# A two-layer gated cross-attention and top-2 expert kernel: expert blocks that start beside the tail of the routing

## The chip, the cores and the metric

One core of one Trainium2 chip runs the whole program. The metric is device time in microseconds of one execution. A profile of one execution gives the time of every instruction on TensorE (PE, its weight loads PEld), VectorE (DVE), ScalarE (ACT), GpSimd (POOL) and of the DMAs that SyncE (SP) and POOL issue.

## What is computed

The input x has 2,048 tokens (8 batches of 256) of width 256; each batch has 120 context rows. Two layers follow each other, cut here to what matters:

```python
for l in range(2):
    x = x + tanh(g_xattn[l]) * cross_attention(layernorm(x), ctx)   # 16 heads of depth 16
    h = layernorm(x)
    w, idx = top_k(softmax(h @ router_w[l]), 2)                     # 8 experts, 2 for each token
    # layer 0: experts silu(h @ gate) * (h @ up) @ down, hidden 688
    # layer 1: experts square(relu(h @ w1)) @ w2, hidden 256
    x = x + tanh(g_ffn[l]) * sum(w[k] * expert[idx[k]](h) for k in range(2))
```

## The kernel before, in words

All arithmetic is f32, but for the rank products and some mask products in bf16. Each layer has an attention part, then an expert part.

**Attention** runs over 16 units (`u`, half a batch of 128 queries each; `G = 16 l + u`). In a unit PE makes the query-ordered scores of the next unit (`scores`), DVE takes row maxima of them (`row_max`, `split_max`, line 841), PE makes the key-ordered scores less the maxima (`shifted`, L1265, L1270), ACT takes their exponent (L647, L649), PE multiplies with the values (`values`, L1291, in two halves), DVE turns and divides (`divide`, L858 to L869), PE projects (`out_proj`, L1299, L1300), DVE adds to x and takes statistics (`residual`, L875 to L881), POOL and ACT normalize (L514 to L519, L657).

**Routing** follows a few units behind: PE transposes the normalized rows (`x2_t`, L1306), ACT copies them out (L663), PE makes 8 logits for each token (`route`, L1312), and for a batch (two units) DVE finds the two experts (`route1`, L893 to L910), PE counts ranks within each expert (`ranks`, L1319 to L1328), DVE makes the row of each token (`route2`, L916 to L930), and POOL scatters the rows of x to a buffer in HBM sorted by expert (`scatter`, L544, four DMAs of a batch). The scatter of batch b stands in POOL's order at unit 2(b+3).

**The list of blocks.** The expert part works through 39 blocks of 128 sorted rows. After the batches 0 to 5 (`EARLY = 6`) `N1 = 17` blocks are sure to be full, whatever the last two batches bring; `list_full` (14 DVE instructions, L995 to L1024) lists their rows and weights, and stands behind the attention loop. `list_rest` lists the other 22 beside the first blocks. The rows between the end of an expert's rows and the next multiple of 128 are filled by eight pad writes (L410), which need the final counts.

**A block** is: SP loads 128 rows (`load_block`, L397, L398, into one of three buffers), PE transposes them (`block_t`, L1468), DVE copies them out (`x_evac`, L1115, L1118), PE multiplies up (`up`, L1482), ACT and DVE apply the nonlinearity (L723 and L1145 in layer 0, L742 and L1172 in layer 1), PE transposes (L1495, L1503) and multiplies down (`down`, L1512), the result is copied out (L1129 or L737), and POOL stores it to the row of each token (`store_block`, L551). The three buffers make the load of block j wait for the transposes of block j-3. At the end of a layer SP reads the results back and DVE adds them to x (`combine`, L825).

Every engine works through its instructions in the order in which they are written; semaphores alone tie the engines together. Between the attention loop and the first block every engine has a piece of code of its own for the last units: on PE, behind the loop (`G1` is the last unit, `B1` the last batch):

```python
route(G1 - 2, 5); x2_t(G1 - 1); out_proj(G1); ranks(B1 - 1)
route(G1 - 1, 7); x2_t(G1); route(G1, 0); ranks(B1)
...
block_t(0)
run_blocks(l, (blk0, blk1)[l])
```

and SP waits for the list, for the scatters of batches 0 to 5 and then loads three blocks. The last expert's weights of layer 0 (slot 7 of `w_all`, where keys and values lie during attention) are loaded once `values` of the last unit is done.

## Time and profile before

| | us |
|---|---|
| median of 3 timed runs (762.58 to 766.7) | 766.17 |
| the profiled execution, its time | 769.0 |
| its span in the profile | 767.3 |
| PE busy | 678.0 (88%) |
| DVE busy | 415.0 (54%) |
| ACT busy | 274.4 (36%) |
| POOL busy | 214.4 (28%) |
| mean granted TensorE clock, share of full | 0.952 |

The span is the time from the first to the last record. Busy shares are averages over parts with different limits, so the two changes from attention to experts have to be read in the timeline, by the waits that end last there. TensorE's clock has two levels here, 2.4 GHz (1.00 in the views) and 1.2 GHz (0.50).

### The profile page before, as it was taken

What the parts mean: (1) busy time and instruction counts of PE and PEld (TensorE: products, weight loads), DVE (VectorE), ACT (ScalarE), POOL (GpSimd) and SP (SyncE); (2) the same over time, 40 slices, a digit from 0 to 9 for tenths busy, and PEclk for the clock granted to TensorE, in tenths of its full rate; (3) what the DMA queues carried; (4) which work ended last, traced back from release to release, by engine and by line L of the source; (5) the groups of instructions that cost most, each with busy time, mean ns of one, the idle gap of its engine ahead of it and who ended that gap; (6) DMA issues with size and microseconds to landing.
All of it is one profiled execution on the core that took longest, in us unless ns stands there. A gap on an engine that the chain in (4) does not pass through costs nothing.

```text
span 767.3 us, 17444 instructions
## 1 busy us (share of the span) xinstructions
PE 678.0 (88%) x5804; PEld 520.4 (68%) x5804; DVE 415.0 (54%) x1385; ACT 274.4 (36%) x528; POOL 214.4 (28%) x399
## 2 busy tenths in 40 slices
PE   5798999859999999999999999978888885999970
PEld 3666767637777777777777777657666663788850
DVE  4777888753333333233332332469989876454426
ACT  3556576411211112112111112256555541354530
POOL 4122553460111111111111011212355436344440
PEclk9999999859999999999999999999999986899995
DMA  9044554461131131111011010320112122544428
GB/s 218 18 144 138 182 179 141 148 220 43 56 101 51 36 79 35 35 32 39 28 35 36 29 28 21 143 92 29 58 64 70 64 85 78 151 125 121 123 83 328
DMA packets 50856, 70.71 MB, mean 92 GB/s; under 512 B 7687, under 2 KB 38023, under 8 KB 50771
## 3 DMA queue, kind: packets, MB, share of 16 engines
q1 hardware_dynamic: 42380, 50.85, 22.1%
q0 software_dynamic: 6816, 18.69, 6.9%
q8 instruction: 51, 0.84, 0.5%
q10 hardware_dynamic: 1575, 0.05, 0.1%
q14 instruction: 34, 0.28, 0.1%
HBM read 46.55 MB, written 23.02 MB: 91 GB/s over the span
## 4 chain that ended last, share of the span: by engine, by line
PE 69%; DVE 18%; issue 5%; DMA 4%; POOL 2%; ACT 2%; DVEq 0%; SPq 0%; POOLq 0%; ACTq 0%
PE ps L1482 28%; PE ps L1512 17%; PE ps L1299 4%; DVE m_rows L841 4%; PE ps L1495 3%; DVE x_sb L825 3%; PE ps L1312 2%; PE ps L1237 2%; DVE ctx_q L858 2%; PE ps L1468 2%; PE ps L1291 2%; DMA ys_dram<-share,dest_i 2%; PE ps L1265 2%; PE ps L1254 1%; DVE x_sb L875 1%
## 5 line engine op out<-in xcount | busy, mean ns | idle before, releaser
L1482 PE MATMUL ps<-w_all,share 128*128 x780 | 232.4, 446 | 4.2 <-DVE share L1118 4.2
L1482 PEld LDWEIGHTS ps<-w_all,share 128*128 128x128 f32 x780 | 146.9, 193 | 66.5 <-issue 8.4
L551 POOL DMA_INDIRECT ys_dram<-share,dest_i x78 | 75.9, 974 | 333.2 <-DVE share L1129 279.8
L1512 PE MATMUL ps<-w_all,share 112*128 (+1 forms) x624 | 147.9, 380 | 1.7 <-ACT share L737 1.0
L1512 PEld LDWEIGHTS ps<-w_all,share 112*128 112x128 f32 (+1 forms) x624 | 112.4, 190 | 15.1 <-issue 2.6
L1145 DVE TENSOR_TENSOR share<-share,ps 128x344 f32<-128x344 f32 x78 | 40.0, 513 | 140.5 <-PE ps L1482 79.3
L726 ACT COPY share<-ps 128x512 f32<-128x512 f32 x39 | 22.9, 587 | 151.9 <-PE ps L1495 151.9
L841 DVE TENSOR_REDUCE m_rows<-ps 128x8 f32<-128x960 f32 x64 | 70.4, 1139 | 11.0 <-PE ps L1254 10.9
L723 ACT ACTIVATE share<-ps 128x344 f32<-128x344 f32 x78 | 35.9, 460 | 106.9 <-PE ps L1482 106.9
L544 POOL DMA_INDIRECT xs_dram<-xn,slot_now x64 | 63.7, 996 | 21.9 <-issue 14.6
L514 POOL TENSOR_SCALAR nm<-mv 128x1 f32<-128x1 f32 (+1 forms) x48 | 12.4, 257 | 162.7 <-DVE mv L881 116.8
L1129 DVE COPY share<-ps 128x256 f32<-128x256 f32 x39 | 16.6, 426 | 68.3 <-PE ps L1512 68.3
L1265 PE MATMUL ps<-q_flat,w_all 32*120 32x256 f32 x512 | 42.1, 413 | 8.2 <-DVE ctx_q L858 6.2
L647 ACT ACTIVATE share<-ps,mask_col 120x1024 f32<-120x1024 f32 x32 | 33.9, 1111 | 26.1 <-PE ps L1270 26.0
L1299 PE MATMUL ps<-w_att,cT 128*128 128x256 f32 x128 | 39.8, 438 | 1.4 <-DVE m_rows L841 0.9
L1115 DVE SCALAR_TENSOR_TENSOR xid<-share,be 128x1 f32<-128x1 f32 x78 | 17.3, 222 | 42.4 <-PE ps L1468 42.0
L1254 PE MATMUL ps<-w_all,q_flat 32*128 32x120 f32 x1024 | 35.6, 275 | 4.9 <-ACT q_flat L629 4.2
L1254 PEld LDWEIGHTS ps<-w_all,q_flat 32*128 32x128 f32 x1024 | 33.1, 186 | 8.3 <-issue 6.6
L1237 PE MATMUL ps<-share,w_att 128*128 128x256 f32 x128 | 34.3, 393 | 3.4 <-issue 2.5
L649 ACT ACTIVATE share<-ps 120x1024 f32<-120x1024 f32 x32 | 31.0, 1020 | 14.3 <-PE ps L1270 14.3
L629 ACT ACTIVATE q_flat<-ps,bq,qs 128x256 f32<-128x256 f32 x64 | 32.5, 565 | 8.9 <-PE ps L1237 8.8
L1468 PEld LDWEIGHTS ps<-ident,share 128*128 128x128 f32 x156 | 22.5, 146 | 15.8 <-issue 2.6
(202 smaller groups left out, 991.3 us busy)
## 6 DMA issues: line engine op xcount, KB each, us to landing
share<-xs_dram SPq DMA_DIRECT2D x78, 129.0 KB, 2.1
w_all<-ys_dram SPq DMA_DIRECT2D x16, 512.0 KB, 7.2
w_all<-gate SPq DMA_DIRECT2D x8, 688.0 KB
w_all<-up SPq DMA_DIRECT2D x8, 688.0 KB
w_all<-down SPq DMA_DIRECT2D x8, 560.0 KB
w_all<-w SPq DMA_DIRECT2D x16, 256.0 KB
xs_dram<-q_flat SPq DMA_DIRECT2D x17, 129.0 KB, 2.4
out<-x_sb SPq DMA_DIRECT2D x8, 256.0 KB, 5.6
```

What stands on the lines that cost most here:

```text
L544: g.indirect_dma_start(xs_dram, bass.IndirectOffsetOnAxis(ap=slot_now[:, B % 2, t, k:k + 1], axis=0), xn2[:, s + t, :], None).then_inc(sca ...
L551: g.indirect_dma_start(ys_dram, bass.IndirectOffsetOnAxis(ap=dest_i[:, u:u + 1], axis=0), y_sb[:, u, :], None).then_inc(D_y[u], 16)
L723: a.activation(act_sb[:, 344 * q:344 * q + 344], ps[:, 2 * q, 0:344], ACT.Silu).then_inc(e_act, 1)
L841: v.tensor_reduce(m_part[:, 2 * h:2 * h + 2, 0:4], ps[:, 2 * h:2 * h + 2, 0:4 * K].rearrange("p g (j k) -> p g j k", j=4), X, ALU.max).the ...
L1145: v.tensor_tensor(h_sb[:, 344 * q:344 * q + 344], act_sb[:, 344 * q:344 * q + 344], ps[:, 2 * q + 1, 0:344], ALU.mult).then_inc(e_h, 1)
L1237: i = t.matmul(ps[:, bank, 0:S], w_att[:, 0, k, m * P:(m + 1) * P], xn1T[:, k, :], start=(k == 0), stop=(k == KT - 1))
L1254: i = t.matmul(ps[:, g, j * K:(j + 1) * K], qT[rows, f, j // 2, j % 2, qt * P:(qt + 1) * P], kT_all[rows, b, j // 2, :], start=(l == 1), s ...
L1265: t.matmul(ps[0:K, 4 + g, 2 * m * P:2 * (m + 1) * P].rearrange("p (e q) -> p e q", e=2), kT_all[rows, b, m, :], qT[rows, f, m, :, qt * P:( ...
L1299: t.matmul(ps[:, 1, 0:D], cT[:, G % 2, k, :], w_att[:, 3, k, :], start=(k == 0), stop=False)
L1468: i = t.transpose(ps[:, 7, k * P:(k + 1) * P], xg[:, j % U3, k * P:(k + 1) * P], ident[:, :])
L1482: i = t.matmul(ps[:, bank, 0:w], xgT[:, k, :], w_all[:, bass.ds(off + (k * UPW[l] + col - EW[l]), w)], start=(k == 0), stop=(k == KT - 1))
L1512: i = t.matmul(ps[:, 6, 0:D], hT[0:r, c + KD[1] * (j % 2) * l, :], w_all[0:r, bass.ds(off + (KT * UPW[l] + c * D - EW[l]), D)], start=(c = ...
```

## The change

1. `EARLY` is 5 instead of 6: 13 instead of 17 blocks are listed early, 26 instead of 22 late.
2. `list_full` is cut in two pieces, which stand on DVE behind `divide` of units 13 and 14, inside the attention loop.
3. The first block's load is issued as soon as the list, the scatters of batches 0 to 4 and the last query projection are done; its transposes stand on PE between the two halves of `values` of the last unit. The buffers for blocks and the scratch of the routing get other places, so that they don't overlap what attention still uses.
4. The routing of the last units (three `route`, two `x2_t`, one `out_proj`, two `ranks` on PE, with their DVE and ACT parts) is no longer ahead of the blocks but between the products of blocks 0 to 3 (layer 0) or 0 to 5 (layer 1).
5. On POOL the eight scatter DMAs of the last two batches stand between the first nine stores of results. On SP the eight pad writes stand behind the loads of blocks up to 9, three pads between two loads, and no longer one behind each of the block loads 3 to 10.
6. The last expert's weights of layer 0 get a semaphore of their own, and PE waits for them at block 4 only.
7. Eight bf16 products of 480 columns, which nobody reads, stand ahead of `shifted` of the last unit of each layer, and two ahead of `shifted` of each even unit from 2 on in layer 1.
8. The exponents of the routing weights and `top_weights` move: in layer 0 to the last block and behind it, in layer 1 the exponents to block 7.

The diff, cut to its core:

```diff
-    EARLY = 6
+    EARLY = 5
...
-        xg = share[:, 0:at_x].rearrange("p (u d) -> p u d", u=U3)
+        xgT = share[:, 2144:2400].rearrange("p (k n) -> p k n", k=KT)
+        xg = share[:, 2400:2400 + U3 * DX].rearrange("p (u d) -> p u d", u=U3)
+        xn2T_last = q_flat[:, 1280:1280 + KT * P].rearrange("p (k n) -> p k n", k=KT)
...
@@ SP
+                for b in range(EARLY):
+                    sp.wait_ge(*scattered(NB * l + b))
+                sp.wait_ge(p_q, 2 * NB * (l + 1))
+                for j in range(2):
+                    load_block(j)
+                if l == 0:
+                    sp.wait_ge(p_pv[1], NU)
+                    load_expert(sp, 0, NE - 1)
+                sp.wait_ge(d_c, NU * (l + 1))
+                for j in range(2, N1 - 3):
                     load_block(j)
                 sp.wait_ge(d_pad, l + 1)
                 sp.wait_ge(g_z, 2 * l + 2)
                 for e in range(NE):
-                    load_block(U3 + e)
+                    if e % 3 == 0:
+                        load_block(N1 - 3 + e // 3)
                     row = sp.value_load(pad_i[0:1, e:e + 1], min_val=0, max_val=NE * REGION - P)
...
@@ POOL
+                token_numbers(B6)
+                scatter_rows(B6, 0, 0)
+                scatter_rows(B6, 0, 1)
+                store_block(l, 0)
+                scatter_rows(B6, 1, 0)
+                store_block(l, 1)
+                scatter_rows(B6, 1, 1)
+                for j in range(2, 6):
+                    store_block(l, j)
+                token_numbers(B7)
+                scatter_rows(B7, 0, 0)
+                store_block(l, 6)
...
+                store_block(l, 8)
+                scatter_rows(B7, 1, 1)
+                for j in range(9, BLOCKS):
                     store_block(l, j)
...
@@ DVE
+                    if u == NU - 1:
+                        x_evac(0)
                     divide(G)
...
+                    if u >= NU - 3 and u < NU - 1:
+                        list_full(u - NU + 3)
...
+                def beside1(j):
+                    if j == 0:
+                        residual(G1)
+                        logits_copy(G1 - 2, LAST_LOGITS[l][0])
+                        route1(B1 - 1)
+                    if j == 1:
+                        route2(B1 - 1)
+                    if j == 2:
+                        logits_copy(G1 - 1, LAST_LOGITS[l][1])
+                    if j == 4:
+                        logits_copy(G1, LAST_LOGITS[l][2])
+                        route1(B1)
+                    if j == 5:
+                        top_shift()
+                    if j == 6:
+                        route2(B1)
+                        counts_done()
+                    if 7 <= j <= 9:
+                        for part in range(3):
+                            list_rest(3 * (j - 7) + part)
...
@@ PE
+                def idle_products(n, bank):
+                    for _ in range(n):
+                        t.matmul(ps[:, bank, 0:4 * K], ident_b[:, :], sel_rows[:, :, :].rearrange("p j k -> p (j k)"),
+                                 start=True, stop=True)
...
+                    if u == NU - 1:
+                        idle_products(8, 7)
+                    elif l == 1 and even and u >= 2:
+                        idle_products(2, 7)
...
+                    if u == NU - 1:
+                        block_t(0)
                     values(G, 1)
...
@@ PE, blocks of layer 0
+                    if j == OTHERS:
+                        t.wait_ge(L_last, 64)
+                    if j == 0:
+                        route(G1 - 2, LAST_LOGITS[l][0])
+                    if j == 1:
+                        last_ranks(B1 - 1)
+                        route(G1 - 1, LAST_LOGITS[l][1])
+                    if j == 2:
+                        route(G1, LAST_LOGITS[l][2])
+                    if j == 3:
+                        last_ranks(B1)
                     up(j, offs[j])
+                    if j == 0:
+                        x2_t(G1 - 1)
+                        out_proj(G1)
+                        t.wait_ge(d_lg, G1 - 1)
+                    if j == 1:
+                        t.wait_ge(e_hTv, 1)
+                        x2_t(G1)
...
```

In the blocks of layer 1 PE has, behind `up(0)`, `route(G1 - 2)` and `x2_t(G1 - 1)`, then `block_t(1)` and `out_proj(G1)`; behind block 1's transposes `last_ranks(B1 - 1)` and `route(G1 - 1)`; in block 3 `x2_t(G1)`, in block 4 `route(G1)` and in block 5 `last_ranks(B1)`.

On DVE, in layer 1, from `divide` of unit 13 (whose last row is the transpose to `cT`) to the next unit's row maxima. Before:

```order
L858 STREAM_TRANSPOSE ctx_q<-ps 128x512
L860 RECIPROCAL recT<-ctx_q 128x16
L863 TENSOR_TENSOR share<-ctx_q,recT 128x2x8x16
L869 STREAM_TRANSPOSE cT<-share 128x256
L841 TENSOR_REDUCE m_rows<-ps 128x2x4 x2
```

Now, the same place:

```order
L929 STREAM_TRANSPOSE cT<-share 128x256
L998 TENSOR_TENSOR share<-cnt_early,thr 128x128
L1001 TENSOR_REDUCE share<-share 128x8
L1003 TENSOR_TENSOR share<-lower,share 128x64
L1005 TENSOR_REDUCE share<-share 128x8
L1007 TENSOR_TENSOR share<-jrow,share 128x104
L1009 TENSOR_SCALAR share<-share 128x8
L1011 TENSOR_REDUCE be<-share 128x13
L1013 SCALAR_TENSOR_TENSOR used<-share 128x8
L901 TENSOR_REDUCE m_rows<-ps 128x2x4 x2
```

Eight instructions of the list now stand between the division and the row maxima; the other six stand behind the division of unit 14.

On PE, in layer 1, from the second half of `values` of the last unit. Before, the last rows of the routing and the first of the blocks are:

```order
L1323 MATMUL ps<-cumb,ones 128x8
L1326 MATMUL ps<-cumb,ones 128x8
L1327 MATMUL ps<-maskb,ones 128x8
L1328 MATMUL ps<-maskb,ones 128x8
L1468 MATMUL ps<-ident,share 128x128 x2
L1521 TENSOR_LOAD woff_i
```

Now (L1389 is `values`, L1435 the transposes of a block, L1591 `up`, L1411 `route`, L1404 `x2_t`, L1397 `out_proj`):

```order
L1389 MATMUL ps<-share,w_all 32x128 x8
L1435 MATMUL ps<-ident,share 128x128 x2
L1389 MATMUL ps<-share,w_all 32x128 x8
L1404 MATMUL ps<-ident,xn 128x128 x2
L1640 TENSOR_LOAD woff_i
...
L1591 MATMUL ps<-w_all,share 128x256
L1411 MATMUL ps<-wr,share 128x8 x2
L1404 MATMUL ps<-ident,xn 128x128 x2
L1435 MATMUL ps<-ident,share 128x128 x2
L1397 MATMUL ps<-w_att,cT 128x256 x2
```

The first block's transposes stand within `values`, and its products ahead of the routing products.

## Rows read from the trace of the kernel before

**Rows 1.** The page, part 2: granted clock of PE in 40 slices of the span.

```profile
PEclk9999999859999999999999999999999986899995
```

**Rows 2.** Chain of waits, 140 to 172 us: start, length, engine and tile.

```profile
157.00 5.26 DMA xs_dram<-xn,slot_now
...
163.31 2.41 DMA share<-xs_dram
```

**Rows 3.** Timeline of PE, layer 0: start, length, operation, idle before and its releaser.

```profile
144.07 1.22 PE L1265 MATMUL ps<-q_flat,w_all 32*120 32x256 f32 x8 [1.74 <-DVE ctx_q L858]
...
167.33 6.82 PE L1482 MATMUL ps<-w_all,share 128*128 x16 [0.81 <-DVE share L1118]
...
175.53 4.79 PE L1482 MATMUL ps<-w_all,share 128*128 x16
```

**Rows 4.** Timeline of PE, layer 0, two units before the last: ranks, scores, logits, projection.

```profile
134.02 0.17 PE L1320 MATMUL ps<-cumb,ones 128*128 128x8 bf16 x1
...
136.94 0.62 PE L1265 MATMUL ps<-q_flat,w_all 32*120 32x256 f32 x8
...
139.09 0.61 PE L1312 MATMUL ps<-wr,share 128*128 128x8 f32 x4 [0.83 <-DVE m_rows L841]
139.56 1.11 PE L1299 MATMUL ps<-w_att,cT 128*128 128x256 f32 x4
...
140.51 0.27 PE L1300 MATMUL ps<-bo_rows,ones 128*128 128x256 bf16 x1
```

**Rows 5.** Stretches: length, PE busy, granted clock, DMA share, GB/s.

```profile
142.00:144.00 2.00, 0.33 (x2) 0.98 0.64 204
144.00:146.00 2.00, 1.93 (x24) 0.50 0.03 8
...
568.00:570.00 2.00, 2.00 (x9) 0.50 0.00 0
```

**Rows 6.** Timeline of DVE, layer 0: first and last of the list, and its middle.

```profile
157.56 0.28 DVE L995 TENSOR_TENSOR share<-cnt_early,thr 128x128 f32<-128x128 f32 x1
...
159.37 0.30 DVE L1012 TENSOR_TENSOR share<-share 128x136 f32<-128x136 f32 x1
...
160.34 0.17 DVE L1024 TENSOR_SCALAR woff_i<-be 128x17 int32<-128x17 f32 x1
```

**Rows 7.** Timeline of PE, layer 1: end of attention, blocks 0, 2, 3 and 13.

```profile
635.72 0.44 PE L1306 MATMUL ps<-ident,xn 128*128 128x128 f32 x2
...
650.43 2.07 PE L1482 MATMUL ps<-w_all,share 128*128 x4 [0.80 <-DVE share L1118]
...
660.36 1.03 PE L1482 MATMUL ps<-w_all,share 128*128 x4
...
683.33 1.03 PE L1482 MATMUL ps<-w_all,share 128*128 x4
```

**Rows 8.** Timeline of SP, layer 1: a block's load and a pad write.

```profile
650.93 0.34 SPq L398 DMA_DIRECT2D share<-xs_dram  x1
652.03 0.36 SPq L410 DMA_DIRECT2D xs_dram<-q_flat  x1
```

**Rows 9.** Timeline of DVE, layer 1, block 8: one of nine parts of `list_rest`.

```profile
672.17 0.54 DVE L1070 TENSOR_REDUCE q_flat<-q_flat 128x22 f32<-128x374 f32 x1
...
672.85 0.15 DVE L1124 TENSOR_TENSOR dest_i<-xid,spare 128x1 int32<-128x1 f32 x1
```

**Rows 10.** The page, part 6: DMA issues, count, KB each, us to landing.

```profile
share<-xs_dram SPq DMA_DIRECT2D x78, 129.0 KB, 2.1
...
xs_dram<-q_flat SPq DMA_DIRECT2D x17, 129.0 KB, 2.4
```

**Rows 11.** Row maxima of DVE in layer 1, starts of units: two of them frame a pair.

```profile
549.27 2.18 DVE L841 TENSOR_REDUCE m_rows<-ps 128x8 f32<-128x960 f32 x2
...
565.57 2.18 DVE L841 TENSOR_REDUCE m_rows<-ps 128x8 f32<-128x960 f32 x2
...
583.28 2.19 DVE L841 TENSOR_REDUCE m_rows<-ps 128x8 f32<-128x960 f32 x2
```

More of the change, by code:

```diff
@@ L382, in _ @@
             for l in range(2):
[L383 to L384 removed]
+                for e in range(NE - 1 if l == 0 else NE):
+                    sp.wait_ge(p_o, NU * l + min(1 + 2 * e, NU - 3))
                     if l == 0 and e == NE - 2:
@@ L726, in blk0 @@
                     a.copy(hT[:, 0:4, :], ps[:, 4, 0:4 * P].rearrange("p (c n) -> p c n", c=4)).then_inc(e_hT, 1)
+                    if first:
+                        ln2_apply(G1)
+                    if last:
+                        top_exp()
                 def hT_evac(j):
@@ L1146, in blk0 @@
                                         ps[:, 2 * q + 1, 0:344], ALU.mult).then_inc(e_h, 1)
+                    if first:
+                        residual(G1)
                     if not last:
@@ L1158, in blk0 @@
                         y_evac(j)
-                    beside(j)
+                    beside0(j)
                 def blk1(j, u, first, last):
-                    if first:
-                        x_evac(j)
                     if j >= 2:
@@ L1540, in blk1 @@
                     up(j, offs[j])
+                    if j == 0:
+                        route(G1 - 2, LAST_LOGITS[l][0])
+                        x2_t(G1 - 1)
+                    if j == 3:
+                        t.wait_ge(d_o, G1 + 1)
+                        x2_t(G1)
                     if not last:
                         block_t(j + 1)
+                    if j == 0:
+                        out_proj(G1)
                     if j >= 1:
```

332 lines of the change are left out of this document (188 added, 144 removed).

## The prediction

> **What bounds the kernel now.** I read the granted clock over the span first, then the chain of waits at the first change from attention to experts, then PE's timeline there, then the same place in layer 1. PE is the bound of the blocks: `up` of layer 0 starts every 8.1 us with no idle time behind it, and of layer 1 ten blocks take 683.33 - 660.36 = 23.0 us, with the clock full [rows 1, 7]. In attention DVE and PE take turns. What the change goes at lies between the two: in layer 0 PE has finished the last unit near 151.4 and starts the first block's products at 167.33 [rows 3], in layer 1 it has finished near 635.7 and starts them at 650.43 [rows 7]. The reader is to see in the chain that this gap ends with a scatter of batch 5, 5.26 us long, and the block's load, 2.41 us [rows 2]: it is latency of a list and of DMAs, and PE's few routing products in it take some 5 us. The granted clock falls with the idle time: it is 0.98 in 142 to 144, where PE is busy for 0.33 of 2 us, and 0.50 in the next 2 us [rows 5]. So `up(0)` takes 6.82 us instead of 4.79 [rows 3], and block 0 of layer 1 takes 2.07 for what takes 1.03 later [rows 7].
>
> **The change part by part.** All places are in the time of the profile before; the sum is made against its own 769.0, which is 2.8 above the median of 766.17.
>
> *List in the loop.* The first eight instructions of the list take 159.37 - 157.56 = 1.8 us, the last six 160.5 - 159.4 = 1.1 [rows 6]. DVE goes from `divide` of unit 13 straight to the row maxima on which PE waits (0.83 us idle for them even now [rows 4]), so the first piece is paid: +1.8, and 0.1 for the copy of the counts, in each layer. The second piece follows `divide` of unit 14, where DVE waits for PE's projection: nothing, as long as that cover is there. With 13 blocks instead of 17 the pieces are a little shorter; I leave that out.
>
> *Idle products.* PE waits 1.74 us for `divide` ahead of the last `shifted` [rows 3]. A bf16 product of 256 columns takes 0.27 and one of 8 takes 0.17 [rows 4], so 480 columns add some 0.2 us each, an estimate from these: eight are 1.6 and fit. They cost nothing while the clock is full; at 0.50 they are 3.2 and push the last unit by up to 1.5. Their gain: `shifted` took 1.22 per eight where it takes 0.62 at full clock [rows 3, 4].
>
> *Layer 0.* `shifted` of the last unit starts at 144.1 + 1.9 = 146.0, its 1.4, then logits, projection and ranks, 1.9, and half of `values`, 0.5, are done at 149.9 at full clock [rows 4]. Meanwhile `divide` of unit 14 ends at 147.1, the list at 148.3; SP takes 1.05 from a wait to a block's load, and the load 2.41 [rows 2], so the rows land at 151.7. The transposes stand there on PE, so the other half of `values` waits: PE idle for 1.8. Batch 4's scatter is issued until 142.3; if it lands in 5.3 it is no later than the list. Transposes 0.4, `values` 0.6, the evacuation 0.7, logits 0.6: `up(0)` starts at 154.1 instead of 167.33. It takes 4.7 at full clock; then come `x2_t`, the projection, the next transposes, `h_t0`, ranks and logits, 3.0 together, and `up(1)` starts at 161.8. Before it was 175.53 [rows 3]: **-13.7**. Behind it one `x2_t`, one `route`, one `ranks`: **+1.0**. The weights of the last expert are wanted at block 4, at about 187, some 30 us after their issue: nothing. Scatters among the stores cost nothing either here, since a block takes 8.1 us. **Layer 0: -12.7.**
>
> *Layer 1.* By the same steps `up(0)` starts at 637.4 instead of 650.43. Now a block is only 2.17 us, and what stood ahead of the blocks must fit between them. Block 2's load waits for `divide` of unit 15, which costs 1.2 us in block 1; the ranks of batch 6 wait for `residual` and `route1` on DVE, 0.6; `route1` of the last batch delays the copy-out in block 5. Blocks 7 to 9 carry nine parts of `list_rest`; one takes 672.85 - 672.17 = 0.7 [rows 9], so three are 2.1 beside DVE's own 1.3, more than a block's 2.17: +1.0 in each of these three blocks, and `top_weights` with 1.4 in block 10. I come to `up(13)` ready on PE at 672.8. But block 13 is in the late list: its load waits for all pads and for the last batch's scatter. The counts are ready at 658.5, in block 6. From there SP issues three loads and eight pads at 652.03 - 650.93 = 1.1 us each [rows 8]: the last pad goes out at 670.6 and lands 2.4 later, the load takes 1.0 on SP and 2.1 [rows 10], transposes and copy-out 1.1: `up(13)` at 677.2, a new wait of 4.4. POOL's order gives nearly the same: the last scatter stands behind the store of block 8 and goes out at about 669. For its landing the chain shows 5.26 under load [rows 2], and I take 3.5, between that and the 2.1 to 2.4 of the other DMAs [rows 10]; the ends move it by 1.8 and 1.4. Against 683.33: **-6.1**. With such a wait the clock falls again, as at 144; from the low level three blocks and their waits took 660.36 - 650.43 = 9.9 us instead of 6.5 [rows 7], so I take **+2.6** for it (ends 0 and 3.4). **Layer 1: -3.5.**
> The Trainium skill (DMA: Bandwidth & Descriptors, Anatomy of one DMA) gives 2.0 us plus the bytes over 436 GB/s for a transfer that POOL issues, 2.3 here, an estimate; the trace's chain has more than twice that, and by the page's price POOL's side would never be last and SP's pads alone would set the wait.
>
> *Dips in layer 1.* The clock is also 0.50 in 568 to 570 [rows 5]. The pair of units around it takes 583.28 - 565.57 = 17.7 us, the one before 16.3 [rows 11]: the two products at even units are worth 1.4 there, if they hold the clock. There is a like dip near 602; I take one of two: **-1.4** (ends 0 and -2.8).
>
> *The longer idle time at unit 14.* The first piece of the list makes PE wait 0.8 + 1.9 = 2.7 us for row maxima in each layer. 1.74 us was followed by the low level at 144, and 0.8 wasn't [rows 3, 4, 5]. If the clock falls, the projection on the chain is 1.5 us longer and the idle products cost up to 1.5 more. Between 0 and 3.0 for a layer I take 1.0, as the wait is nearer to the first row: **+2.0**.
>
> Moved exponents and `top_weights` (1.4 us) lie, in layer 0, under the store and the reading back, some 6 us of latency in which DVE waits: nothing. Sum: -12.7 - 3.5 - 1.4 + 2.0 = **-15.6**, so 753.4 for the profiled execution and **750.6** for the median.
>
> **The rivals.**
> 1. *The clock goes the other way.* Activity is thin at unit 14, in the new wait within the last `values`, and in the early blocks of layer 1. If it is at 1.2 GHz in all of these, the last unit is 1.9 slower in each layer, `up(0)` of layer 0 2.0, some three early blocks of layer 1 take 3.2 instead of 2.17, the 3.0 at unit 14 is paid in full, and the dips stay: 4.4 + 4.6 + 1.4 = 10.4 more, **761**. For it: every idle stretch over 1.7 us in the rows is followed by 0.50. Against: the products fill one of them.
> The Trainium skill (TensorE: Matmul & The Clock Gate, HAM oscillation) has this as a rule, that waits between bursts throttle the array again and again; the rows at 144 and 568 agree.
> 2. *Nothing waits at block 13.* If the early blocks run somewhat later than I reckon or the pads go faster, the wait is hidden and the clock stays: 4.4 + 2.6 less, and 2.0 less at unit 14: **741.6**.
> 3. *The first block is not early.* If batch 4's scatter lands late beside the weight loads of expert 6, the second half of `values` waits, and with it everything. Four us in each layer and the clock with it make **760**. Against: the weights' bytes have ended by 144 (204 GB/s in 142 to 144, then 8 [rows 5]).
> 4. *Slower than before.* Blocks of layer 1 that wait for DVE, for buffers, for pads and for scatters between stores keep PE at the low level. A block is then (660.36 - 650.43) / 3 = 3.3 instead of 2.17. Beyond the 2.6 already taken it has to last for more than (766.2 - 750.6 + 2.6) / 1.14 = 16 blocks to be slower than before; with all 39 it is 792. Against: before, PE came out of it after three blocks [rows 7].
>
> **How the numbers follow.** Forecast 0.50 (746 to 755), rival 1 0.22, rival 2 0.19, rival 3 0.06, rival 4 0.03. The range takes rivals 2, 3 and 1 in: 741 to 761. A measurement of this kernel can tell 0.5%, 3.8 us, from no change, so faster is below 762.3. Rival 1 lies close to that bound, and a fifth of its chance goes beyond: faster 0.88, within 0.5% 0.08, slower 0.04.
>
> **What would show it.** Row maxima of unit 15 later by 1.9 behind the list in both layers; granted clock 1.00 through the last unit; `up(0)` of layer 0 some 13 us earlier relative to `divide` of unit 12 and 4.7 long; in layer 1 `up(0)` 13 us earlier and a wait of about 4 us ahead of `up(13)`, released by its load. The prediction is wrong in a step if block 13 doesn't wait, if the clock is at 0.50 in the last unit or over more than four blocks, or if PE waits longer than 2 us between the two halves of the last `values`.

## The result: a third of the forecast gain, and the profile after

| | before | after |
|---|---|---|
| median | 766.85 us (759.92 to 770.81, 20 runs) | 761.96 us (755.81 to 766.73, 20 runs) |
| profiled execution | 769.0, span 767.3 | 764.07, span 762.3 |
| ratio | | 0.9936, 95% interval 0.9915 to 0.9958 |

The change makes the kernel faster by 0.64%, 4.9 us. The forecast was 15.6 us, and 761.96 lies just outside the range of 741 to 761. Run again, on a chip of the same speed, the changed kernel took 0.9939 (e5 below). So the direction was right and two thirds of the gain are missing.

The page of the changed kernel, granted clock and DMA share in 40 slices of 19 us, is to be read beside [rows 1]:

```profile
PEclk9999999899999899999999999999999999979995
DMA  9044564451124411011011000421122223534429
```

There is a new slice with 8 in the middle of the blocks of layer 0 (the 14th, near 260 us), where before nothing happened. The timeline of PE shows it. First the end of attention in layer 0, which answers to [rows 3, 4] (columns: start, length, operation, count, idle time before and its releaser):

```profile
141.35 0.96 PE L1411 MATMUL ps<-wr,share 128*128 128x8 f32 x4 [2.56 <-DVE m_rows L901]
142.16 2.05 PE L1397 MATMUL ps<-w_att,cT 128*128 128x256 f32 x4
...
146.81 2.51 PE L1441 MATMUL ps<-sel_rows,ident_b 128*128 128x480 bf16 x8
149.25 0.71 PE L1363 MATMUL ps<-q_flat,w_all 32*120 32x256 f32 x8
...
153.44 0.44 PE L1435 MATMUL ps<-ident,share 128*128 128x128 f32 x2 [0.48 <-DMA share<-xs_dram]
```

And the same engine around block 13 of layer 0:

```profile
253.74 4.79 PE L1591 MATMUL ps<-w_all,share 128*128 x16
263.51 0.69 PE L1435 MATMUL ps<-ident,share 128*128 128x128 f32 x2 [4.98 <-DMA share<-xs_dram]
263.99 4.61 PE L1631 MATMUL ps<-w_all,share 128*128 x12
268.44 0.82 PE L1610 MATMUL ps<-ident,share 128*128 128x128 f32 x6
269.10 4.79 PE L1591 MATMUL ps<-w_all,share 128*128 x16
```

`up(12)` starts at 253.74 and `up(13)` at 269.10: 15.36 us for a block that takes 8.1 before it and behind it. PE waits 4.98 us for block 13's rows, and L1631, the down products, then takes 4.61 instead of 2.76 us. Before, `up(13)` of layer 0 started at 272.73. So of the lead of 11.9 us that `up(1)` had (163.60 against 175.53 [rows 3]), 3.6 us are left one block after 12. The windows (length, PE, weight loads, DVE, ACT, POOL busy, granted clock, DMA share, GB/s) show the wait, the DMA engines busy all through it (share 1.06 and 1.11), and the clock on its lower level of 1.2 GHz (0.50) behind it:

```profile
258.00:260.00 2.00, 0.53 (x2) 0.00 (x0) 0.51 (x1) 0.00 (x0) 0.00 (x0) 1.00 1.06 241
260.00:262.00 2.00, 0.00 (x0) 0.00 (x0) 0.00 (x0) 0.00 (x0) 0.00 (x0) 0.73 1.11 228
262.00:264.00 2.00, 0.49 (x3) 0.49 (x4) 0.00 (x0) 0.00 (x0) 0.00 (x0) 0.50 0.58 136
264.00:266.00 2.00, 2.00 (x6) 1.64 (x6) 0.62 (x3) 0.00 (x0) 0.00 (x0) 0.50 0.03 8
```

What ends the wait stands in the timelines of DVE and of SP's queue:

```profile
254.34 0.60 DVE L1156 TENSOR_REDUCE q_flat<-q_flat 128x26 f32<-128x442 f32 x1
254.98 0.18 DVE L1158 SCALAR_TENSOR_TENSOR xrow_i<-q_flat 128x26 int32<-128x26 f32 x1
255.08 0.32 DVE L1160 TENSOR_SCALAR woff_i<-be 128x26 int32<-128x26 f32 x1
```

```profile
255.50 1.08 SPq L377 DMA_DIRECT2D q_flat<-ctx  x2
257.59 2.75 SPq L413 DMA_DIRECT2D share<-xs_dram  x3
```

The late list, `list_rest`, is done at 255.4. SP, which waits for it, issues first the two loads of layer 1's context (480 KB each) and only then block 13's load. In the chain of waits (L445 is SP's wait for the list, L377 a context load) that load takes 5.87 us, against 2.41 in [rows 2]:

```profile
255.43 0.03 SPq L445
255.45 0.04 issue
255.50 0.39 SPq L377
...
257.59 5.87 DMA share<-xs_dram
```

Before, the context loads stood in the same order, at 271.49, but the first block behind them was block 17, far from its turn. With five batches in the early list instead of six its last block is 12, and the late list serves block 13.

In layer 1 the forecast mechanisms are all there. Its timeline of PE, to be read beside [rows 7]:

```profile
635.26 1.13 PE L1591 MATMUL ps<-w_all,share 128*128 x4 [0.25 <-issue]
...
640.69 0.44 PE L1435 MATMUL ps<-ident,share 128*128 128x128 f32 x2 [1.46 <-DMA share<-xs_dram]
...
669.12 0.44 PE L1435 MATMUL ps<-ident,share 128*128 128x128 f32 x2 [2.46 <-DMA share<-xs_dram]
...
670.53 2.07 PE L1591 MATMUL ps<-w_all,share 128*128 x4
674.84 0.69 PE L1435 MATMUL ps<-ident,share 128*128 128x128 f32 x2 [2.24 <-DMA share<-xs_dram]
...
677.45 1.91 PE L1591 MATMUL ps<-w_all,share 128*128 x4
```

`up(0)` starts at 635.26 instead of 650.43, and `up(13)` at 677.45 instead of 683.33, behind waits of 2.46 and 2.24 us for the loads of blocks 12 and 13, 4.7 together where the prediction had 4.4 at block 13 alone. Block 12 is in the early list, but its load stands behind six of the pads on SP. The 3.5 us by which layer 1 starts earlier (first row maxima at 503.02, before 506.51) are in these differences.

### The profile page after: what moved, and what is told of

It is laid out like the page before. It is cut to its first block, busy times and chain, and to the rows that moved or that the text cites. A ratio compares the mean times of both kernels' runs of the same rounds, so it can differ in the third digit from the quotient of the medians.

```text
span 762.3 us, 17516 instructions
## 1 busy us (share of the span) xinstructions
PE 681.4 (89%) x5834; PEld 519.7 (68%) x5834; DVE 415.2 (54%) x1385; ACT 273.0 (36%) x528; POOL 213.2 (28%) x399
## 4 chain that ended last, share of the span: by engine, by line
PE 70%; DVE 17%; DMA 5%; issue 4%; ACT 1%; SPq 1%; POOL 0%; DVEq 0%; POOLq 0%; ACTq 0%
PE ps L1591 27%; PE ps L1631 18%; PE ps L1397 4%; DVE m_rows L901 4%; PE ps L1610 3%; DVE x_sb L885 3%; DMA share<-xs_dram 2%; PE ps L1435 2%; PE ps L1335 2%; PE ps L1411 2%; DVE ctx_q L918 2%; PE ps L1389 2%; PE ps L1352 2%; PE ps L1363 2%; PE ps L1313 1%
## 5 line engine op out<-in xcount | busy, mean ns | idle before, releaser
L1591 PE MATMUL ps<-w_all,share 128*128 x780 | 229.9, 442 | 1.7 <-DVE share L1039 0.8
L1591 PEld LDWEIGHTS ps<-w_all,share 128*128 128x128 f32 x780 | 145.1, 191 | 62.0 <-issue 3.6
L579 POOL DMA_INDIRECT ys_dram<-share,dest_i x78 | 75.6, 970 | 321.3 <-DVE share L1199 271.3
L1631 PE MATMUL ps<-w_all,share 112*128 (+1 forms) x624 | 151.1, 386 | 1.8 <-ACT share L789 1.0
L1631 PEld LDWEIGHTS ps<-w_all,share 112*128 112x128 f32 (+1 forms) x624 | 114.9, 194 | 15.7 <-issue 2.6
L1435 PE MATMUL ps<-ident,share 128*128 128x128 f32 x156 | 30.9, 281 | 13.5 <-DMA share<-xs_dram 13.5
L1435 PEld LDWEIGHTS ps<-ident,share 128*128 128x128 f32 x156 | 21.7, 144 | 28.7 <-DMA share<-xs_dram 16.5
L1397 PE MATMUL ps<-w_att,cT 128*128 128x256 f32 x128 | 39.1, 432 | 0.3 <-DVE m_rows L901 0.2
```

Of the source, the lines that this page charges most:

```text
L579: g.indirect_dma_start(ys_dram, bass.IndirectOffsetOnAxis(ap=dest_i[:, u:u + 1], axis=0), y_sb[:, u, :], None).then_inc(D_y[u], 16)
L1397: t.matmul(out_psum(G), cT[:, G % 2, k, :], w_att[:, 3, k, :], start=(k == 0), stop=False)
L1435: i = t.transpose(ps[:, 2 if j == 0 else 7, k * P:(k + 1) * P], xg[:, j % U3, k * P:(k + 1) * P], ident[:, :])
L1591: i = t.matmul(ps[:, bank, 0:w], xgT[:, k, :], w_all[:, bass.ds(off + (k * UPW[l] + col - EW[l]), w)], start=(k == 0), stop=(k == KT - 1))
L1631: i = t.matmul(ps[:, 6, 0:D], hT[0:r, c + KD[1] * (j % 2) * l, :], w_all[0:r, bass.ds(off + (KT * UPW[l] + c * D - EW[l]), D)], start=(c = ...
```

## The experiments

Sixteen runs followed, of 13 different kernels, on four chips. They are of two speeds: on one chip the kernel before takes 766 us (e5 to e8, and the result above was on such a chip), on the three others 796 to 798 (e1 to e4, e9 to e12, e13 to e16). Ratios are each to the kernel before on the same chip, from 4 to 6 executions (e5 from 12). Context loads are those of L377.

| run | speed of the chip | median us | ratio, 95% interval |
|---|---|---|---|
| e5 changed kernel | 766 | 761.36 | 0.9939 (0.9916 to 0.9963) |
| e6 context loads late | 766 | 754.48 | 0.9845 (0.9810 to 0.9881) |
| e7 and list behind unit 14, bridged | 766 | 753.32 | 0.9833 (0.9798 to 0.9867) |
| e8 e6 and layer 1's pads, scatters | 766 | 752.30 | 0.9809 (0.9774 to 0.9844) |
| e13 changed kernel | 796 | 789.85 | 0.9891 (0.9859 to 0.9922) |
| e1 context loads late | 796 | 779.87 | 0.9789 (0.9763 to 0.9815) |
| e2 late list early | 796 | 780.06 | 0.9784 (0.9758 to 0.9809) |
| e12 both | 796 | 778.56 | 0.9789 (0.9764 to 0.9814) |
| e3 changed, no unread products | 796 | 790.11 | 0.9915 (0.9895 to 0.9935) |
| e10 e1, no pairs in layer 1 | 796 | 781.84 | 0.9831 (0.9814 to 0.9849) |
| e11 e1, none in the last units | 796 | 782.69 | 0.9808 (0.9771 to 0.9846) |
| e14 e1, none at all | 796 | 785.70 | 0.9831 (0.9801 to 0.9861) |
| e4 changed, list behind unit 14 | 796 | 794.17 | 0.9978 (0.9954 to 1.0001) |
| e9 e8, list bridged in layer 0 | 796 | 781.89 | 0.9809 (0.9786 to 0.9833) |
| e15 the same as e9 | 796 | 782.80 | 0.9802 (0.9772 to 0.9832) |
| e16 e12 and e8 | 796 | 779.99 | 0.9763 (0.9730 to 0.9797) |

### Block 13 of layer 0: e1, e2, e5, e6, e12, e13

e1 and e6 move the context loads behind three block loads:

```diff
                 sp.wait_ge(d_l2, 19 * (l + 1))
+                for j in range(N1, N1 + 3):
+                    load_block(j)
                 if l == 0:
                     load_ctx(0)
                     load_ctx(1)
-                for j in range(N1, BLOCKS):
+                for j in range(N1 + 3, BLOCKS):
                     load_block(j)
```

e2 leaves SP alone and ends the late list four blocks earlier:

```diff
-                    if 3 <= j <= 11:
-                        list_rest(j - 3)
+                    if 3 <= j <= 7:
+                        for part in range(2 * (j - 3), min(9, 2 * (j - 3) + 2)):
+                            list_rest(part)
```

e12 does both; e5 and e13 are the changed kernel as it is.

> The changed kernel, but in layer 0 the two loads of 480 KB of context rows stand on SP behind the loads of blocks 13 to 15, not ahead of them. Theory A (block 13 of layer 0 waits because its load is behind and beside the context rows, 5.87 us to landing instead of some 2.4): PE's idle time ahead of its transposes falls from 4.98 us to about 0.5, the clock stays at 1.00 there, up(12) to up(13) falls from 15.4 to about 8.6, time 6.5 us under the changed kernel, about 755. Theory B (it waits because the late list is finished only in block 11, at 255.4, whatever stands ahead of the load): idle time stays above 3 us and the time falls by less than 3.

> The changed kernel, but in layer 0 list_rest goes two parts to a block in blocks 3 to 7 instead of one in blocks 3 to 11. Theory A and theory B both give back the whole wait here, since list and context rows are done some 10 us ahead of block 13's load: no idle time ahead of its transposes, up(12) to up(13) 8.1, time about 7.3 us under the changed kernel, 754.5. If the wait stays, it is the scatter of the last batch between the stores (theory C) that holds the load.

> The changed kernel, unchanged, beside the three edits below on one chip, as their yardstick. On the first chip it took 0.9936 of the kernel before. On the chip of the first four experiments the kernel before took 796 us instead of 767. If the change loses its gain in layer 0 mostly through the wait at block 13, this run stands 7 to 11 us above e6 and shows the idle time of 5 us ahead of block 13's transposes again; if the slower chip alone made the first two edits look good, it stands within 3 us of e6.

> The same edit as e1: in layer 0 SP issues the two context loads behind the loads of blocks 13 to 15 instead of ahead of them. Theory (the 480 KB of context ahead of block 13's rows on the same queue make its load land 5.9 us after issue): up(12) to up(13) in layer 0 falls from 15.4 to 8.1 us, so 7.3 us less than e5, ratio to before about 0.984. Rival (the late list is what block 13 waits for, wherever the context loads stand): up(12) to up(13) stays over 12 us and the time stays that of e5.

> As e6, and the late list of layer 0 in two parts per block in blocks 3 to 7, so that it is done four blocks earlier. Theory (list end and context loads each alone would have removed the wait, and what is left of it in e6 is 0.4 to 0.5 us ahead of block 13's transposes): no idle time there, 0.5 us less than e6, no difference that five rounds can tell. Rival (the list's operations, two parts per block, delay the gating on VectorE in blocks 3 to 7): blocks 3 to 7 take over 8.1 us each, and the time is above e6.

On the faster chip e6 stands 6.9 us under e5, and PE's timeline of e6 at block 13 has, where e5 has an idle time of 5.00 us:

```profile
254.05 4.79 PE L1593 MATMUL ps<-w_all,share 128*128 x16
259.26 0.44 PE L1437 MATMUL ps<-ident,share 128*128 128x128 f32 x2 [0.42 <-DMA share<-xs_dram]
259.54 2.78 PE L1633 MATMUL ps<-w_all,share 128*128 x12
262.16 0.82 PE L1612 MATMUL ps<-ident,share 128*128 128x128 f32 x6
262.82 4.79 PE L1593 MATMUL ps<-w_all,share 128*128 x16
```

From 254.05 to 262.82 are 8.8 us, where e5 has 14.9 (255.23 to 270.10) and the first profile 15.4. The chain of waits of e6 has the load of block 13 as

```profile
257.18 2.04 DMA share<-xs_dram
```

so it goes out 1.4 us behind the end of the list (255.7) and takes 2.0. In the changed kernel it goes out 2.2 us behind it and takes 5.87: 0.7 us of the wait are SP's time for issuing the context loads, 3.8 are the transfer behind and beside them. In e2, where the context loads stay ahead and only the list is earlier, `up(12)` starts at 263.64 and `up(13)` at 271.74, 8.1 us, with no idle time between. In e12 the same place, with the late list early as well, has no idle time either (the last row is cut off by the end of the window):

```profile
263.84 4.79 PE L1594 MATMUL ps<-w_all,share 128*128 x16
268.47 0.38 PE L1438 MATMUL ps<-ident,share 128*128 128x128 f32 x2
268.69 2.76 PE L1634 MATMUL ps<-w_all,share 128*128 x12
271.29 0.82 PE L1613 MATMUL ps<-ident,share 128*128 128x128 f32 x6
271.94 4.50 PE L1594 MATMUL ps<-w_all,share 128*128 x15
```

e1, e2 and e12 agree in time to 0.2%: it takes both, a list that ends 3 us ahead of its first use and 960 KB ahead of the load on the queue, to make the wait, and undoing either removes it. That 0.5 us of e12 cannot be told. The ratios of e1 and e2 were better than I expected, and it looked as if the cause were larger than block 13. It was the speed of the chip: the changed kernel on such a chip (e13) is at 0.9891.

> The changed kernel, unchanged, again as the yardstick of this call. If the chip is the one on which the kernel before takes 766 us: 0.994 of it. If it is the slower one: theory (the wait at block 13 costs 7 us on either chip, and e1 stood at 0.9789 without it) 0.987 to 0.989; rival (the slower chip itself gains more from the early blocks) 0.980 or less.

So the order of SP's loads is worth 6.9 us on the faster chip, where both ran side by side, and 1.0%, 8 to 10 us, on the slower ones, where e1 and e13 ran on different chips; e13's profile has an idle time of 4.11 us at block 13, and 23.0 us from block 12's to block 14's transposes (260.56 to 283.53) where 16.2 are two blocks.

### The early list between units 13 and 14: e4, e7

e4 puts the whole list behind the division of unit 14; e7 does so on top of e6 and bridges the wait for block 0 with eight more unread products:

```diff
-                    if u >= NU - 3 and u < NU - 1:
-                        list_full(u - NU + 3)
+                    if u == NU - 2:
+                        list_full(0)
+                        list_full(1)
...
                     if u == NU - 1:
+                        idle_products(8, 2)
                         block_t(0)
```

> The changed kernel with all 14 instructions of the early list behind the division of unit 14; none behind that of unit 13. Theory (the first piece makes PE wait 2.56 us for row maxima in layer 0 and the clock falls there): idle time ahead of the logits of unit 14 goes back to 0.8 us, the clock is 1.00 from 138 to 146, division of unit 14 ends 3.5 us earlier in layer 0 and some 2.5 in layer 1; the list then ends 1.5 to 3 us earlier in each layer, and so does the start of the first block; time 2 to 5 us under the changed kernel. Rival: the list stays the last thing that the first block waits for and takes 2.9 us there, so all is given back within the last values, and the time is the same within 1 us.

> As e6, and in both layers the whole early list stands behind the divide of unit 14 (as in e4), with eight more unread products, 120 columns x 4 each as in the last unit, ahead of block 0's transposes within the last unit's value products. Theory (what a late list costs at either place is the fall of the granted clock that follows a wait of over 2 us, and products that bridge the wait keep the clock): idle time ahead of unit 14's routing back to 0.9 us, its projection 1.1 instead of 2.05 us, the wait ahead of block 0 of 3.2 us down to under 1 us, clock at full speed into up(0); layer 0 some 2 us and layer 1 some 1 us shorter than e6. Rival (the products only take the place of the wait and the list is the limit at its length of 3.9 us): the same time as e6 within 1 us. Third (the clock falls all the same, as in e4): 2 to 3 us above e6.

In e4 the wait for row maxima at unit 14 goes back to 0.85 us, the projection of unit 14 to 1.11, and the load of block 0 comes late in its stead. PE's timeline of e4:

```profile
152.29 0.61 PE L1412 MATMUL ps<-wr,share 128*128 128x8 f32 x4 [0.85 <-DVE m_rows L901]
152.76 1.11 PE L1398 MATMUL ps<-w_att,cT 128*128 128x256 f32 x4
...
165.68 0.44 PE L1436 MATMUL ps<-ident,share 128*128 128x128 f32 x2 [3.21 <-DMA share<-xs_dram]
...
169.13 7.32 PE L1592 MATMUL ps<-w_all,share 128*128 x16
```

and of e7, where the eight products fill part of it:

```profile
148.02 1.79 PE L1444 MATMUL ps<-sel_rows,ident_b 128*128 128x480 bf16 x8
151.37 0.44 PE L1438 MATMUL ps<-ident,share 128*128 128x128 f32 x2 [1.56 <-DMA share<-xs_dram]
...
153.68 4.87 PE L1595 MATMUL ps<-w_all,share 128*128 x16
```

The list in one piece without a bridge is 0.9978, 0.9% above e13: the split that the change makes is the better place, and my expectation for e4, 2 to 5 us less, fell. Bridged, `up(0)` starts at 153.68 instead of 156.07 (e6), at full clock, 2.4 us earlier. In layer 1 the clock fell all the same (0.50 in 624 to 628), and the time as a whole is that of e6 within its interval (0.9833, 0.9845). The profile shows where the lead goes: in layer 1 `up(0)` of e7 starts 5.9 us ahead of e6 (622.36 against 628.27), `up(13)` only 1.5 (667.14 against 668.60), behind new waits of 2.54 and 1.88 us for blocks 12 and 13. On the slower chips e9 and e15, with the bridge in layer 0 alone, are no better than e1. So the bridged place is worth 1.2 us in the medians of e6 and e7, and no run shows that it is worth anything clear of the noise.

### The unread products: e3, e10, e11, e14

e3 leaves out both lines of the loop that call `idle_products`, e14 does so on top of e1, e10 leaves out the pairs of layer 1 alone, e11 the eight of each last unit alone:

```diff
-                    if u == NU - 1:
-                        idle_products(8, 7)
-                    elif l == 1 and even and u >= 2:
-                        idle_products(2, 7)
```

> The changed kernel without any of the products that nobody reads (eight ahead of the last key-ordered scores of each layer, two at even units of layer 1). If they hold the clock, as the prediction had it, the last unit of each layer is at 0.50 and the low level comes more often in attention of layer 1: 2 to 5 us slower than the changed kernel. Rival: in the changed kernel the clock had fallen before them, at unit 14, and they themselves took 2.51 us at the low level in layer 0; then leaving them out costs nothing or gains up to 2 us.

> As e6, without the two unread products of each even unit of layer 1; the eight of each last unit stay. My prediction had the pairs at -1.4 us, because they would hold the clock through layer 1's attention. Theory from the trace of the changed kernel (the clock dips there all the same): 6 pairs take 0.58 us each where no wait is bridged, so without them the time falls by up to 3 us or stays. Rival (they hold the clock in most units): 2 us or more longer than e6.

> As e6, without the eight unread products of the two last units; the pairs of layer 1 stay. With e10 it splits the 1.3 per cent that e3, without any of them, stood above e1. Theory (the eight hold the clock through the last unit, where without them it stays at 1.2 GHz after the wait of unit 14): up(0) in layer 0 1 us later and in layer 1 1 to 3 us later, 3 to 6 us above e6. Rival (they only fill a wait that is there anyway, and the pairs carried the rest): within 1.5 us of e6.

> The context loads of layer 0 behind the loads of blocks 13 to 15, and no unread products anywhere. Theory (together the products are worth the 0.4 per cent of e10 and what e11 lost): 0.3 to 0.8 per cent longer than the context-late kernel with products (0.9789 on the slower chip, 0.9845 on the other), so 0.983 to 0.987 on the slower one or 0.988 to 0.992 on the other. Rival (the clock falls in attention with or without them, and they only take time): no longer, or shorter by up to 2 us.

Against the kernels with all products on chips of the same speed (e1 and e12, both 0.9789), e14 is 0.42% above, e10 0.42%, e11 0.19%; with block 13's wait in place e3 is 0.24% above e13. e10, e11 and e12 ran on one chip: e10's difference to e12, 3.3 us, is just larger than the noise of two such ratios, 0.3%, and e11's is well inside it, so the 3 to 6 us that I expected of the eight products fell. All four point the same way, and together they make it likely that the products are worth 2 to 3 us, more of it in the pairs of layer 1 than in the last units. What the pairs hold is not seen in a single unit: the clock falls in units with them too. In layer 1 of the changed kernel:

```profile
580.00:584.00 4.00, 3.14 (x27) 2.38 (x18) 2.65 (x6) 1.94 (x2) 0.00 (x0) 0.72 0.00 0
```

and between the first and the last row maxima of layer 1's attention nine profiles with pairs on the slower chips took 123.9 to 131.2 us at a mean granted clock of 0.93 to 0.97, three without them 129.2 to 131.1 us at 0.91 to 0.93. That the pairs make the falls rarer fits this, but the ranges meet, and it is not shown. My expectation for e10, no gain or a loss from the pairs, fell.

### Layer 1, block 13: e8, e9, e15, e16

e8 is e6 with the late part of layer 1 reordered on three queues: the last batch's four scatters ahead of the stores of blocks 6 to 8, and four of eight pads from ScalarE's queue. The edit as it is in layer 1 (the conditions on `l` that keep layer 0 as it was are left out on GpSimd):

```diff
@@ sync
-                for e in range(NE):
+                for e in range(NE if l == 0 else NE // 2):
...
+                if l == 1:
+                    load_block(N1 - 1)
@@ gpsimd, layer 1
                 scatter_rows(B7, 0, 0)
-                store_block(l, 6)
                 scatter_rows(B7, 0, 1)
-                store_block(l, 7)
                 scatter_rows(B7, 1, 0)
-                store_block(l, 8)
                 scatter_rows(B7, 1, 1)
+                store_block(l, 6)
+                store_block(l, 7)
+                store_block(l, 8)
@@ scalar, blk1
                     if j == 7:
                         top_exp()
+                        a.wait_ge(d_pad, 2)
+                        a.wait_ge(g_z, 4)
+                    if 7 <= j <= 8:
+                        for e in range(NE // 2 + 2 * (j - 7), NE // 2 + 2 * (j - 7) + 2):
+                            row = a.value_load(pad_i[0:1, e:e + 1], min_val=0, max_val=NE * REGION - P)
+                            a.dma_start(xs_dram[bass.ds(row, P), :], zrow).then_inc(D_pad, 16)
```

> As e6, and in layer 1 the last batch's four scatters stand ahead of the stores of blocks 6 to 8 on GpSimd, and four of the eight pads are issued from ScalarE's queue in blocks 7 and 8 (SP issues the other four). Theory (in layer 1 block 13 waits for the last scatter, issued at 667.8, and for pads, of which the last is issued at 668.5, one after another on two queues): loads of blocks 13 to 15 are issued 3 to 4 us earlier, the waits of 2.2 to 2.5 us ahead of blocks 12 and 13 shrink to under 1 us, the clock does not fall to 1.2 GHz there, and the time is 3 to 5 us under e6. Rival (the late list's operations on VectorE, done at 664.6, and what follows are the limit; or ScalarE's issues delay the relu of blocks 8 and 9): within 1.5 us of e6 or above it.

> The edits that each paid where they paid: the context loads behind block 13 to 15's loads (e6), in layer 0 alone the whole early list behind the divide of unit 14 with eight unread products ahead of block 0's transposes (e7), in layer 1 the last scatters ahead of the stores and four pads from ScalarE's queue (e8). If the three gains are independent they add: e7's trace gained 2.3 us in layer 0 over e6, e8 gained about 2 us over e6, so 4 to 5 us under e6, about 0.979 of the kernel before. If layer 1's gain is used up by a wait that an earlier start brings forward, it stands with e8 within 1 us.

> The kernel of e9 again, on the chip of this call. If it is the one of e5 to e8: gains add and it takes 0.978 to 0.980 of the kernel before (e7 0.9833, e8 0.9809), or, if not, 0.981 and over. On the slower one: 0.981 as e9.

> The context loads late, the late list of layer 0 two parts per block (as e12), and in layer 1 the last scatters ahead of the stores and four pads from ScalarE's queue (as e8); the early list and the products as in the changed kernel. If e8's gain of 2 us and e12's half a us add: 0.980 of the kernel before on the chip of e8, 0.976 on the other. If layer 1's wait has come back in another place: as e12 within 1 us.

PE's timeline of e6, blocks 12 and 13 of layer 1:

```profile
662.81 0.44 PE L1437 MATMUL ps<-ident,share 128*128 128x128 f32 x2 [3.06 <-DMA share<-xs_dram]
...
667.22 0.44 PE L1437 MATMUL ps<-ident,share 128*128 128x128 f32 x2 [0.60 <-DMA share<-xs_dram]
```

and of e8:

```profile
661.79 0.44 PE L1452 MATMUL ps<-ident,share 128*128 128x128 f32 x2 [0.33 <-DMA share<-xs_dram]
...
665.04 0.44 PE L1452 MATMUL ps<-ident,share 128*128 128x128 f32 x2 [0.71 <-DMA share<-xs_dram]
```

The waits for blocks 12 and 13 shrink from 3.7 to 1.0 us, and the clock stays at 1.00 from 660 on in e8's windows, where e6 has 0.62 in 664 to 668. Part of it is paid back earlier: ScalarE's two issues take 1.49 us ahead of the nonlinearity of one block and 1.37 ahead of the next, and the wait of PE ahead of `up(10)`, 0.62 us in e6, is 1.52 in e8. What is left is 2.2 us at block 13, although layer 1 starts 1 us later in e8's profile than in e6's, and 2.2 in the median; the intervals of e6 and e8 overlap, so by time alone it is likely and not shown, and it is less than the 3 to 5 us that I expected. e16, which carries the same edit on top of e12, met its expectation of 0.976 (0.9763) and has the lowest ratio on the slower chips, 1.3% under the changed kernel on the same chip; e1, e2 and e12 lie within its interval. e9 and e15 came out at 0.981 and 0.980, no better than e1, which has neither of the two edits that they add to it: the gains do not add. e15 and e16 on one chip differ by 0.4%, inside the noise, so it is likely and not shown that the bridged list is the part to leave out. e8 is the best on the faster chip, 9.1 us under the changed kernel and 13.9 under the kernel before on the same chip.

## Why the prediction missed

The profiled executions differ by 4.9 us where the sum said 15.6. The 10.7 us between them, step by step:

- **Layer 0, `up(0)` and `up(1)`: nearly right.** `up(0)` was put at 154.1 and starts at 155.75, takes 4.87 (forecast 4.7), and `up(1)` starts at 163.60 (forecast 161.8). PE waits 0.48 us between the halves of `values` (forecast 1.8), since it comes there later itself. The gain is 11.9 instead of 13.7; `up(12)` is 10.9 earlier than before, against -11.7 in the sum with the share for unit 14.
- **Layer 0, the step that failed: the late list.** The prediction says of layer 1 that "block 13 is in the late list". For layer 0 it passes over the same fact and says that the scatters among the stores cost nothing "since a block takes 8.1 us". It never asked what stands between the end of `list_rest` at 255.4 and block 13's transposes, which PE could start at 258.5: 3 us of time, and ahead of the load on SP the two context loads. The sum has nothing for it. It costs 7.3 us in the profile (15.36 - 8.1), and e5 against e6 measures 6.9. It alone is two thirds of the miss. Of the cases listed, none had it; rival 4 is of its kind, but in layer 1.
- **The first piece of the list** was put at a wait of 2.7 us for row maxima at unit 14 and measured 2.56 and 1.92. The clock fell in both layers, to 0.50 for 142 to 148 in layer 0, so that the projection took 2.05 instead of 1.11 and the eight products 2.51. The sum had 1.0 for this in each layer, with ends 0 and 3.0. e6 and e7 differ by 2.4 us at `up(0)` of layer 0, of which 1.7 are the shorter wait at unit 14. The 0.7 that remain are no clean measure of the clock, since e7 also waits 0.7 longer for block 0's rows and has eight products more: that the middle of 1.0 was fair is likely and not shown.
- **The unread products** were put at -1.4 us, for one dip of two. A dip is there all the same (0.72 in 580 to 584). Their worth is 2 to 3 us by e3, e10 and e14, likely and about as large as the noise, so the sign holds and the size may be too small; that two products at an even unit hold the clock over a certain dip does not hold. The "granted clock 1.00 through the last unit" that I asked of the profile comes late in layer 0: 0.50 in 146 to 148, when the eight products start, 0.93 in 148 to 150, and 1.00 from there.
- **Attention of layer 1** is 2.4 us longer from its first to its last row maxima (503.02 to 621.19, before 506.51 to 622.25). The sum had +1.9 for the list, -1.4 for the dip and +1.0 for the clock, 1.5. Miss: 0.9.
- **Layer 1, blocks.** The places of the forecast are in the time of the profile before, so 3.5 us have to be added to those of after. `up(0)` is then at 638.8, with the sum at 637.4 - 1.4 + 1.0 = 637.0: 1.8 late, 0.9 of it from attention. `up(13)` is at 680.9 and was put at 677.2, 39.8 us behind `up(0)`; it took 42.2. The wait for the late list is there, on both queues, and each is about 2 us later than forecast: the last scatter goes out at 667.84, so 671.3 (forecast 669), and lands 3.75 later (3.5), the last pad at 672.1 (670.6). Of the 2.6 for the clock 1.9 did not come behind `up(13)`: from there to the last stores only 0.7 is lost (5.9 us ahead at `up(13)`, 5.2 at the first of them, 748.04 against 753.26), since part of it was paid already between blocks 12 and 13, where `up(12)` took 2.07. Together layer 1 gains 1.7 of its own where the sum had 3.5 + 1.4 - 1.0 = 3.9.
- **The scatter's price.** The Trainium skill (DMA: Bandwidth & Descriptors, Anatomy of one DMA) gives 2.3 us for such a transfer by its formula, an estimate; the trace has 3.75 for the one on which block 13 waits. The measurement decides: issued at 667.84, it landed at 671.59. With 2.3 us it would have landed at 670.1, ahead of the last pad (issued by 668.65, and pads take 2.6 us in the middle here), and the pads would have set the wait.
- **The chances.** Faster by over 0.5% came true, barely: 761.96 against the bound of 762.3. Rival 1 names the time, 761, but not the way to it, and that it fits is luck. Of its places the clock was low at unit 14 (142 to 148 in layer 0) and not in `up(0)` of layer 0 (4.87 us) or the early blocks of layer 1 (1.03 to 1.13), and block 13 of layer 0 is not among them. Its sum is wrong besides: the terms as they are listed come to 2 x 1.9 + 2.0 + 3 x 1.03 + 2 x 2.0 + 1.4 = 14.3, not 10.4, so it should have named 765, and the range should have ended there.

Layer 0 missed by 0.8 and 7.3, layer 1 by 2.2: 10.3 of the 10.7. What stays open is how the falls of the clock are spread over attention from run to run; single profiles of the same kernel move `up(1)` of layer 0 by 1.5 us (163.60 and 165.09: `up(0)` takes 6.56 us in e5, where block 0's rows came after an idle time of 1.55, 4.87 in the first profile behind 0.48).

## What to carry to other kernels

When a boundary between an early and a late part moves, every consumer behind it moves too: look up, in each layer, what the first item of the late part waits for and what is queued ahead of it, though the layer's long items seem to hide everything. A bulk load that nobody needs soon goes behind the small load that is needed next, and this reordering of two lines was worth more than the change itself. In these profiles a wait of PE was often paid a second time in the clock (behind 4.98 us a down product took 4.61 instead of 2.76, behind 2.56 a projection 2.05 instead of 1.11), so a wait saved or bridged can be worth more than its length, but only where nothing else is late just behind it: e7's lead of 5.9 us in layer 1 was down to 1.5 at block 13.

## What the runs showed that I had not expected

**Chips of two speeds, 30 us apart.** The kernel before takes 766 us on one and 796 on another, and e6's kernel 754.48 and 779.87 (e1). The bytes are the same and the mean clock nearly (0.975 and 0.969). In e1's table of waits, as in those of all eleven other runs on slower chips and in none from a faster one (e5 to e8, and the two of the result), ScalarE and VectorE wait for a releaser that the view calls remote (columns: us in total, times, longest):

```profile
ACT share L695 <- remote: 25.8, 5, 5.6
...
ACT share L693 <- remote: 23.6, 5, 6.0
...
DVE x_sb L937 <- remote: 17.0, 7, 2.6
```

One of them: at 82.85 the exponent of a unit comes 3.5 us after the scores it needs, behind the loads of an expert's weights (issued until 75.6, DMA share 1.07 in 76 to 80). What is remote there, and whether these waits are the 30 us, no run tells. The changed kernel's gain came out larger on such a chip (0.9891 against 0.9939, with intervals that just touch).

**A small load behind large ones.** Block 13's rows took 5.87 us behind 960 KB on the same queue, where such a load takes 2.1 in the middle [rows 10]; with three block loads ahead of the context it took 2.04, and PE waited 0.42 us (e6) instead of 4.98.

**The clock and the length of a wait.** In layer 0, `up(0)`, 16 products, took 4.87 us where PE had waited 0.48, 0.89 and 0.94 us for block 0's rows (the changed kernel, e6, e1), 6.56 behind 1.55 (e5), 7.32 behind 3.21 (e4, with 1.19 more ahead of the logits), and again 4.87 behind 1.56 where eight products stood just ahead (e7). But e9 has 7.87 with the products and 0.61, behind a second idle time of 1.37 us ahead of the logits: it is not the length of one wait alone. That waits between bursts throttle the array again and again is also what the Trainium skill says (TensorE: Matmul & The Clock Gate, HAM oscillation); these rows agree with it, here behind waits of 1.55 and 3.21 us.
